# Second GATv2 sweep: VectorE adds the second tile's fetched rows in the bank, in place of TensorE's identity product

## The reference

```python
def gatv2_conv(x, src, dst, Wl, Wr, att, b, heads, c_out):
    xl = (x @ Wl).reshape(n, heads, c_out)
    xr = (x @ Wr).reshape(n, heads, c_out)
    e = jax.nn.leaky_relu(xl[src] + xr[dst], NEG_SLOPE)
    logit = jnp.einsum('ehc,hc->eh', e, att)
    m = jax.ops.segment_max(logit, dst, num_segments=n)
    a = jnp.exp(logit - m[dst])
    denom = jax.ops.segment_sum(a, dst, num_segments=n)
    out = jax.ops.segment_sum((a / denom[dst])[:, :, None] * xl[src], dst, num_segments=n)
```

## Time and profile before

| | us |
|---|---|
| three runs | 7316.95, 7317.35, 7345.25 |
| median | 7317.35 |
| profiled execution, own time | 7313.39 |
| its span | 7311.6 |
| PE busy | 5467.1 (75%) |
| DVE busy | 4841.4 (66%) |
| ACT busy | 2775.2 (38%) |
| POOL busy | 3686.8 (50%) |
| L1058, identity products, both GATv2 sweeps | 467.9 in 1856 instructions |

### The profile page before, as it was taken

One profiled execution on the slowest core, in us unless ns is written; L12 is line 12 of the kernel. 1 busy time (PEld: TensorE's weight loads), 2 busy tenths in 40 slices (PEclk: granted clock), 3 DMA queues, 4 the chain that ended last, 5 costly groups with the idle time before them and its releaser, 6 DMA issues. The chain is left out here.

```text
span 7311.6 us, 115062 instructions
## 1 busy us (share of the span) xinstructions
PE 5467.1 (75%) x25450; PEld 4274.3 (58%) x25451; DVE 4841.4 (66%) x13284; ACT 2775.2 (38%) x9159; POOL 3686.8 (50%) x3856
## 2 busy tenths in 40 slices
PE   2788377769998488856777897777987777867775
PEld 1566366747776266645555685555775555734465
DVE  7666267747776566646999657999559997733313
ACT  0111166635666155523444234443334443300025
POOL 0577277726665177714666105665016663367730
PEclk9999989979999577777999998999999999966677
DMA  1000245546555155635777326776237775023330
GB/s 31 3 3 3 38 151 154 152 81 178 174 172 132 54 159 158 154 79 190 224 225 224 75 70 215 226 226 181 71 99 230 226 227 147 14 84 104 105 56 18
DMA packets 453631, 933.98 MB, mean 128 GB/s; under 512 B 109900, under 2 KB 207110, under 8 KB 453126
## 3 DMA queue, kind: packets, MB, share of 16 engines
q0 software_dynamic: 209536, 582.56, 30.2%
q1 hardware_dynamic: 239520, 346.64, 14.5%
q10 hardware_dynamic: 4326, 2.03, 0.1%
HBM read 789.17 MB, written 141.76 MB: 127 GB/s over the span
## 5 line engine op out<-in xcount | busy, mean ns | idle before, releaser
L1099 PE MATMUL bank<-arena,onehots 128*128 128x264 f32 (+3 forms) x6496 | 2002.7, 439 | 232.3 <-DMA arena<-tab_l,slot_src 120.3
L1055 PE MATMUL bank<-arena,spreads 128*128 x5568 | 1480.8, 375 | 599.9 <-DVE raw L1269 345.5
L1015 POOL DMA_INDIRECT arena<-tab_l,slot_typed x1392 | 1317.3, 946 | 719.7 <-issue 300.8
L1099 PEld LDWEIGHTS bank<-arena,onehots 128*128 128x128 f32 x6496 | 1306.9, 221 | 601.3 <-issue 212.0
L1055 PEld LDWEIGHTS bank<-arena,spreads 128*128 128x128 f32 x5568 | 1030.6, 210 | 980.3 <-issue 857.3
L1015 POOL DMA_INDIRECT arena<-tab_l,slot_src x928 | 884.7, 953 | 478.0 <-issue 259.3
L871 ACT ACTIVATE onehots<-iota_row,slot_loc 128x128 f32<-128x128 f32 x1856 | 641.1, 392 | 948.6 <-PE bank L1099 928.5
L1286 DVE TENSOR_TENSOR acc<-acc,bank 128x264 f32 (+3 forms) x1624 | 654.2, 403 | 504.9 <-PE bank L1099 495.1
L1189 DVE TENSOR_TENSOR arena<-arena,bank 128x512 f32<-128x512 f32 x928 | 630.2, 679 | 181.0 <-ACT stats L1137 75.8
L1015 POOL DMA_INDIRECT arena<-tab_l0b,slot_src x464 | 467.5, 1008 | 349.1 <-POOLq L1503 112.9
L1015 POOL DMA_INDIRECT arena<-tab_l0a,slot_src x464 | 453.8, 978 | 279.3 <-POOLq L1503 122.0
(11 more groups left out here) (376 smaller groups left out, 8078.9 us busy)
## 6 DMA issues: line engine op xcount, KB each, us to landing
spreads<-spread_dram SPq DMA_DIRECT2D x580, 256.0 KB
tab_l<-arena SPq DMA_DIRECT2D x150, 384.0 KB, 3.3
spread_dram<-spreads SPq DMA_DIRECT2D x116, 256.0 KB
onehot_dram<-onehots SPq DMA_DIRECT2D x58, 512.0 KB, 3.7
onehots<-onehot_dram SPq DMA_DIRECT2D x58, 512.0 KB, 4.1
arena<-tab_l,slot_typed POOLq DMA_INDIRECT x1392, 4.1
arena<-tab_l,slot_src POOLq DMA_INDIRECT x928, 2.8
arena<-tab_l0a,slot_src POOLq DMA_INDIRECT x464, 2.6
```

The costliest lines, as they stand in the source:

```text
L1015: pool.indirect_dma_start(out=rows_sb[:, a, t, half:half + width], out_offset=None, in_=table[:, :], in_offset=bass.IndirectOffsetOnAxis(a ...
L1055: mm = pe.matmul(z[x.k % 2][:, t, 0:cw], spreads[:, x.k, t * P:t * P + P], qtab[:, block_no[w], 0:cw], start=True, stop=not gatv2)
L1099: mm = pe.matmul(sums[x.k % 2], onehots[:, x.a, GT * x.k + t, :], rhs, start=t == 0, stop=t == GT - 1)
```

## The change

In the second GATv2 sweep the identity product is left out for the second tile of each pair. VectorE gets a new operation at the head of its slot: it waits for the target products of the pair and for the fetched rows, and adds the rows of the second tile to that tile's half of the bank, in the bank. ScalarE's activation waits for this addition (`joined`) in place of PE's products.

```diff
+            vector_adds = gatv2 and not first
...
                                 mm = pe.matmul(z[x.k % 2][:, t, 0:cw], spreads[:, x.k, t * P:t * P + P],
-                                               qtab[:, block_no[w], 0:cw], start=True, stop=not gatv2)
-                                if gatv2:
+                                               qtab[:, block_no[w], 0:cw], start=True,
+                                               stop=not gatv2 or (vector_adds and t == 1))
+                                if gatv2 and not (vector_adds and t == 1):
                                     mm = pe.matmul(z[x.k % 2][:, t, 0:cw], ident[:, :],
                                                    rows_sb[:, x.a, GT * x.k + t, in0:in0 + cw], start=False, stop=True)
...
-                            act.wait_ge(S["target_spread"].sem, S["target_spread"].at(x.g + 1))
+                            z_made = S["joined"] if vector_adds else S["target_spread"]
+                            act.wait_ge(z_made.sem, z_made.at(x.g + 1))
...
                         if x.there and oh_dve:
                             one_hots(dve, x)
+                        x = Group(i, w, LAG["target"])
+                        if x.there and vector_adds:
+                            dve.wait_ge(S["target_spread"].sem, S["target_spread"].at(x.g + 1))
+                            dve.wait_ge(arrived[x.a][x.k].sem, arrived[x.a][x.k].at(32 * (x.use + 1)))
+                            dve.tensor_tensor(z[x.k % 2][:, 1, 0:cw], z[x.k % 2][:, 1, 0:cw],
+                                              rows_sb[:, x.a, GT * x.k + 1, in0:in0 + cw], ALU.add)\
+                               .then_inc(S["joined"].sem, 1)
                         xl = Group(i, w, LAG["logit"])
```

More of the change, by code:

```diff
@@ L820, in gnn_kernel @@
         att = sb("att", [P, 2 * D])
-        names = ("oh_made", "oh_turned", "spread_made", "target_spread", "activated", "multiplied_rows", "raw_made",
+        names = ("oh_made", "oh_turned", "spread_made", "target_spread", "activated", "joined", "multiplied_rows", "raw_made",
                  "logits_made", "logits_turned", "mid", "cols_made", "cols_spread", "shifted_made", "powers_made",
@@ L1359, in edge_pass @@
             if gatv2:
-                per_group += ("activated",)
+                per_group += ("activated",) + (("joined",) if vector_adds else ())
             if hgt or gatv2:
```

## The result

| | before | after |
|---|---|---|
| median of five runs of each, us | 7316.95 (7307.75 to 7345.25) | 7386.85 (7382.30 to 7392.51) |
| profiled execution: own time, span | 7313.39, 7311.6 | 7382.33, 7380.5 |
| ratio | | 1.0091, 95% interval 1.0069 to 1.0113 |

The change makes the kernel 0.9% slower, some 69 us. The forecast was 7373 in 7325 to 7418: the direction is right, and the time is 14 us short, inside the range. In the changed kernel the lines behind L1055 are shifted: the new addition is L1206, the logits copy L1333, the identity product L1060, `head_rhs` L1314.

What follows compares the result with a forecast made beforehand. PE was taken to bound ordinary slots, with one wait for VectorE's `head_rhs` per batch. Order +30 and clock +26 gave +56 us on 7313.39, thus 7369; the median lies 4 above: 7373, range 7325 to 7418.

Steps and rivals of the forecast that it cites:

- The bound and the regimes: Second GATv2 sweep: PE fills a batch's eight slots, and once per batch of eight pairs waits for VectorE's `head_rhs`.
- E10 to E11: From the end of slot 10's target products (logits copied there) to slot 11's: 4.10 us, before 2.72, lost 1.38.
- E11 to L1314's end: From the end of slot 11's target products to `head_rhs` ready: 7.60 us, before 6.93, lost 0.67.
- L1314 to E14: From `head_rhs` ready to the end of slot 14's target products: 2.80 us, before 3.24, won 0.44.
- E14 to E16: From the end of slot 14's target products to slot 16's: 5.22 us, before 5.34, won 0.12.
- E16 to E18: Two ordinary slots, from slot 16's target products' end to slot 18's: 4.91 us, before 5.23, won 0.32.
- The order's term: Batch chain with VectorE waiting behind PE: 24.63 against 23.46 us, +1.17 per batch, 30 us over 26 batches.
- The clock's term: PE's longer wait for `head_rhs` drops it to half clock: 1.0 us per batch, 26 us over 26 batches.
- Rival A: The sweep's clock holds at 2.4 GHz, so only +30 us: 7347; chance 0.20.
- rival C: Clock falls behind nearly every wait and stays low longer, 7 us per batch: +98 us, 7415; chance 0.15.
- The two batches left out: Of the sweep's 28 batch intervals, two where it fills and drains were not counted, leaving 26.
- Rival B: Addition fits VectorE's idle time, holding up nothing behind it: 36 to 89 us faster, centre 7275; chance 0.09.

Runs made afterwards that it cites:

- e2: Kernel before, both identity products kept, only the wait for the pair's target products put at the head of VectorE's slot; ratio 1.0060, 7374.08 us.
- e9: Changed kernel with both identity products kept; VectorE waits and adds in an unused bank, ScalarE waits for that addition; ratio 1.0160 to the kernel before.
- e10: Changed kernel with the addition moved behind the logits copy in slot 10 and behind the first scans in slot 11; ratio 1.0052 to the kernel before.
- e4: Changed kernel with four unused identity products on PE ahead of the wait for `head_rhs`; ratio 1.0066 to the kernel before, 7378.69 us.
- e3: Kernel before, both products kept, plus a same-shape VectorE addition in an unused bank, waiting for no PE product, nobody waiting for it; ratio 0.9992.
- e1: Changed kernel with the addition taken out and ScalarE's wait put back to PE's products; ratio 0.9947 to the kernel before, 7290.83 us.
- e7: Kernel before with the three operations that make `head_rhs` moved ahead of slot 12's multiply, on a chip where the kernel before took 8722.76 us; ratio 1.0028.

## Why the prediction was right, and by how much it was not

- **The bound and the regimes**: right before the change, by the rows; e2 and e9 show that VectorE's place behind PE, and ScalarE's behind VectorE, is what lengthened the batch at full clock.
- **Removed, added**: 232 products and 232 additions, each 0.43 us long where I took 0.41 from the 264-wide addition; the next instruction starts 0.34 later (1962.33, 1962.67), as taken. The nearest row was the right one to take between 0.20 and 0.69.
- **E10 to E11**: 4.47 against 4.10 forecast (E11 = 1966.65). The hand-over into the addition was 0.15 and not 0.04, the multiply 0.76 and not 0.68, the transpose and the lead up to the products 0.46 and not 0.38, and the products took 1.56 from start to end, not 1.45. The wait at L1033 was forecast at about 1 and was 1.1. e10, which takes the addition out of this link and out of the front of the next, gave 1.11 back, part of it by fewer falls.
- **E11 to L1314's end**: 7.57 against 7.60. The wait was 2.34 where 2.4 was forecast.
- **L1314 to E14**: 4.48 against 2.80: the clock fell here, 1.7 and not the 1.0 put on a batch.
- **E14 to E16**: 5.38 (E16 = 1984.08) against 5.22. **E16 to E18**: 4.90 against 4.91, so ordinary slots are 2.45 as forecast.
- **The order's term was under-sized**: the links without the fall give 26.80 - 1.68 = 25.12 us. Seven of the 28 batches have no fall; the four of them without the loop's turn took 25.04, 25.17, 25.42 and 25.55; the one of before was 23.46. So it is some +1.7 per batch, not +1.17: the 0.37 of E10 to E11 and the 0.16 of E14 to E16. That is the step which failed in size: its hand-overs and durations were read where the trace before had no such chain, and each came out 0.1 us or so longer. Over 26 batches it is some 44 us, not 30.
- **The clock's term**: +26 us was forecast, as 1.0 in each of 26 batches; right in the sum, by two errors that cancel. Batches with a fall are longer than those without: without the loop's turn 26.7 against 25.3, with it 27.8 against 26.65. The wait was the same 2.34 us in both kinds, so the difference is the clock's. 21 of 28 had one: 21 x 1.3 = 27 us, and e4 recovered 24. So a fall cost more than 1.0, and a quarter of the batches had none. Over the sweep's middle the granted clock was 0.95, as forecast from the HGT sweep, which is 2.7 us low per batch (0.05 / 0.5 of 755) where 3 was taken. Rival A, no fall, did not come, and neither did rival C with 7 us low per batch.
- **The two batches left out**: of the 28 intervals the last two took 27.2 and 28.0 before, 28.0 and 26.5 after. The other 26 lost 26.94 - 24.20 = 2.74 each, 71 us, against 2.17 forecast.
- **Rival B**, that the addition fits beside: its condition, the copy no later than 0.5 us behind E10, was missed by two microseconds. e3 shows that its first half was true, the work is hidden as long as it waits for nothing; e2 shows that the wait alone makes the kernel slower. And by e1 its price was at the low end: 35 us, of 36 to 89.

The Trainium skill, "TensorE: Matmul & The Clock Gate", section "HAM oscillation — how this bites in real kernels", tells of waits between bursts that put the array back to half clock. The runs agree in kind: in the changed kernel a fall followed 20 of the 28 waits for `head_rhs`, mostly of 2.34 us (granted clock 0.95). They do not for e2's waits of 1.6 us (1.00). So a wait has to be priced by the clock shown in rows near it.

Open: why seven of the 26 waits of 2.34 us had no fall behind them (the first wait, 3.57 us, had one; the last was 0.43); how the 1.65 us that the addition takes behind its wait split between its length and its two hand-overs; and which of its waits would have to go for e1 to bring the whole 3.44 us. e4's five falls come at other places than `head_rhs`: one behind a wait of 2.1 us for the logits copy and one behind a wait of 0.9 us for it, three where a wait of 1.0 us for ScalarE and the turn of PE's loop, 1.0 us, stand within 2.2 us.

## What to carry to other kernels

An instruction that waits for another engine at the head of an in-order queue costs first of all what stands behind it: here the addition was free without its wait (ratio 0.9992) and the wait dear without the addition (1.0060). Behind such a wait the instruction's own length counts too (1.0160 with both, and the product kept). Before work is moved to a less busy engine, see how far that engine runs ahead of the producer and who consumes what it makes next; where it runs ahead, place the new work behind what others wait for. And price a removed wait or product by the next wait in line: 100 us of PE's work brought 35, and the removal of the largest wait nothing that the times can tell.

## What the runs showed of the hardware

- An addition of 128x256 float32 with the bank as input and output takes 433 ns; one of 264 columns from a bank into SBUF takes 422. The output in the bank costs next to nothing extra.
- The longer PE's idle wait for `head_rhs` in the middle of a busy sweep, the more falls to half clock the 28 batches had: 0 at 1.5 us (before), 1 at 1.6 (e2), 8 at 1.9 (e9), 12 at 2.0 (e10), 22 at 2.34 (the change). Nearly all came within 1.6 us of the wait's end. The length of this wait alone does not decide it: the addition alone (e3) had 1 at 1.5, and e1 and e4, where PE also had other idle waits, had 5 each at 1.3 and 0.6.
- A fall made a batch of the changed kernel 1.2 to 1.4 us longer, and one of e9 1.7 (28.72 against 27.03).
- PE can wait for fetched rows while POOL is not full: in e1, with POOL busy for 429 of 600 us, it did so in 37 of the about 170 slots of 500 us, for up to 2.0 us.
- One chip ran the same kernel in 8722.76 us and not in 7317. In e7's profile there VectorE's busy time was 4861.1 us, in that of the kernel before on the other chip 4841.4, so VectorE's instructions were no slower there; its time went into waits.
